# Two VectorE passes of an attention layer trade places around the z1 remainder

## The reference

```python
def layer(h, p):
    q = _phi(h @ wq + bq_)            # _phi(t) = elu(t) + 1
    k = _phi(h @ wk + bk_)
    v = h @ wv + bv_
    kv = einsum('bshd,bshm->bhdm', k, v)
    z = 1.0 / (einsum('bshd,bhd->bsh', q, k.sum(axis=1)) + 1e-06)
    att = einsum('bshd,bhdm,bsh->bshm', q, kv, z)
    h = _ln(h + att @ wo + bo_, g1_, be1_)
    y = gelu(h @ w1 + c1_) @ w2 + c2_
    return _ln(h + y, g2_, be2_)
xn = _layernorm(x)
out = x + attention_stack(xn) * silu(experts(xn))
```

## Time and profile before

| | us |
|---|---|
| median of three runs | 862.58 (862.35 to 863.84) |
| the profiled execution, device time | 865.69 |
| its span in the trace | 863.9 |
| TensorE busy in the span | 814.1 (94%) |
| VectorE busy | 777.9 (90%) |
| ScalarE busy | 736.0 (85%) |
| GpSimd busy | 407.6 (47%) |

### The profile page before, as it was taken

One profiled execution on the slowest core, in us unless ns is written; L12 is line 12 of the kernel. 1 busy time (PEld: TensorE's weight loads), 2 busy tenths in 40 slices (PEclk: granted clock), 3 DMA queues, 4 the chain that ended last, 5 costly groups with the idle time before them and its releaser, 6 DMA issues.

```text
span 863.9 us, 19249 instructions
## 1 busy us (share of the span) xinstructions
PE 814.1 (94%) x5914; PEld 738.6 (85%) x5914; DVE 777.9 (90%) x2675; ACT 736.0 (85%) x1315; POOL 407.6 (47%) x392
## 2 busy tenths in 40 slices
PE   5698999999999999999999999999999999998837
PEld 4588899999999999999999999999999999987624
DVE  6888999989899899989899899989899899998698
ACT  2579899989998899989999899989998899889734
POOL 5233454445544455344544445344544445465482
PEclk9799999999999999999999999999999999999985
DMA  5300200001010100001010100001010000000011
GB/s 147 89 2 2 44 2 18 18 16 30 2 35 2 44 2 22 14 17 28 2 34 2 45 1 24 12 18 27 2 35 2 1 1 2 12 15 1 2 38 61
DMA packets 26264, 18.76 MB, mean 22 GB/s; under 512 B 4354, under 2 KB 22195, under 8 KB 26164
## 3 DMA queue, kind: packets, MB, share of 16 engines
q1 hardware_dynamic: 25300, 16.95, 7.3%
q10 hardware_dynamic: 864, 0.59, 0.2%
HBM read 15.43 MB, written 2.10 MB: 20 GB/s over the span
## 4 chain that ended last, share of the span: by engine, by line
PE 80%; DVE 10%; ACT 7%; issue 3%; DMA 0%; ACTq 0%; DVEq 0%
PE down_ps L764 20%; PE small_ps L697 6%; PE att_ps L727 6%; PE up_ps L754 5%; PE up_ps L756 5%; PE up_ps L755 5%; PE t_ps L675 5%; PE t_ps L734 4%; PE kq_ps L687 3%; PE kq_ps L688 3%; PE kq_ps L689 3%; DVE z_lo L1042 3%; ACT z_hi L915 2%; PE up_ps L718 2%; PE small_ps L705 2%
## 5 line engine op out<-in xcount | busy, mean ns | idle before, releaser
L764 PE MATMUL down_ps<-w_use,hid 128*128 128x128 f32 x2048 | 259.8, 275 | 1.2 <-DVE h L1007 1.0
L764 PEld LDWEIGHTS down_ps<-w_use,hid 128*128 128x128 f32 x2048 | 244.0, 192 | 2.4 <-issue 2.0
L1060 POOL TENSOR_TENSOR res_ffn<-z_tm,g_ffn 128x512 f32<-128x512 f32 x64 | 81.9, 1279 | 249.4 <-DVE k_e L1173 237.9
L1049 POOL TENSOR_TENSOR res_att<-z_tm,g_att 128x512 f32<-128x512 f32 x64 | 82.5, 1288 | 154.4 <-DVE h L1000 154.4
L866 ACT ACTIVATE hid<-up_ps 128x512 f32<-128x512 f32 x192 | 113.3, 592 | 22.3 <-PE up_ps L756 14.8
L1012 DVE BATCH_NORM_STATS2 st<-h 128x6 f32<-128x128 f32 x504 | 107.1, 273 | 0.1
L921 ACT ACTIVATE z_tm<-h,shift,rstd 128x128 f32<-128x128 f32 x244 | 99.9, 483 | 0.0
L754 PE MATMUL up_ps<-z_hi,w_hi 128*128 128x512 f32 x192 | 86.5, 450 | 3.4 <-ACT hid L866 3.4
L1063 POOL TENSOR_TENSOR res_ffn<-res_ffn,ffn_row 128x512 f32<-128x512 f32 x64 | 84.1, 1314 | 5.0
L1052 POOL TENSOR_TENSOR res_att<-res_att,att_row 128x512 f32<-128x512 f32 x64 | 82.3, 1286 | 5.0
L687 PE MATMUL kq_ps<-w_kq_hi,zq_hi 128*128 128x256 f32 x256 | 82.0, 320 | 1.5 <-DVE zq_lo L958 1.5
(11 more groups left out here) (211 smaller groups left out, 2013.7 us busy)
## 6 DMA issues: line engine op xcount, KB each, us to landing
raw_w<-in_L_attn_W SPq DMA_DIRECT2D x15, 256.0 KB, 4.4
out_y<-gate_tm SPq DMA_DIRECT2D x8, 256.0 KB, 2.0
bias_bc<-in_L_attn_c SPq DMA_DIRECT2D x7, 256.0 KB, 4.7
x_tm<-in_L_attn_x SPq DMA_DIRECT2D x3, 512.0 KB, 7.2
raw_rows<-in_L_attn_be SPq DMA_DIRECT2D x15, 64.0 KB, 4.1
raw_g<-in_L_attn_g SPq DMA_DIRECT2D x14, 64.0 KB, 3.1
x_tm<-in_L_attn_x SPq DMA_DIRECT2D x2, 256.0 KB, 3.3
raw_rows<-in_L_attn_bo SPq DMA_DIRECT2D x8, 64.0 KB, 3.8
```

Source lines behind the costliest of these rows:

```text
L764: last = nc.tensor.matmul(down_ps[:, t, :], hid[:, j, t * P:(t + 1) * P], w2_use[:, j, :], start=(j == 0), stop=(j == FC - 1))
```

## The change

In each step VectorE takes the queries' last pass ahead of the z1 remainder, where the keys' floor pass stood, and the keys' floor pass behind the z1 remainder. No instruction is added or removed, and the lists of the other engines stay as they were.

```diff
@@ -1306,9 +1306,11 @@
                 dve_q_n(dve, p)
                 dve_kvo(dve, p)
             if proj:
-                dve_k_floor(dve, p + 1)
+                dve_q_elu(dve, p + 1)
             if ln1:
                 dve_z1_lo(dve, p - 1)
+            if proj:
+                dve_k_floor(dve, p + 1)
             if b == 1 and in_layers(l, 1, L - 1):
                 dve_w1_lo(dve, l)
             if proj:
@@ -1317,8 +1319,6 @@
                 dve_h2(dve, p - 2, b)
             if in_layers(l, 1, L - 2) and b in ZF_TILES and is_unit(p):
                 dve_zf(dve, l, ZF_TILES[b])
-            if proj:
-                dve_q_elu(dve, p + 1)
             if ffn:
                 dve_stats_of(dve, h2[:, b % 2], TT, s["h2_s"], p - 1, "st2_s")
```

## The result

The changed kernel takes **875.8 us** (median of 4 runs, 875.36 to 876.13); the kernel before, on the same chip, 863.21 (4 runs, 862.35 to 863.97). The ratio is 1.0146, 95% interval 1.0128 to 1.0163: the change costs 12.6 us, where 10.7 were forecast. The profiled execution took 876.13 us, with a span of 874.4, which is 10.5 longer than that of the profiled execution before (863.9).

What follows compares the result with a forecast made beforehand. TensorE was taken to set the time, VectorE counting only where TensorE waits. Six middle layers +6.3, first and last layer +3.0 and start +1.4 made +10.7 us, added to the 862.58 median: 873.3. Range: from rival 1 (865.9) up to 877.

Steps and rivals of the forecast that it cites:

- The floor pass is GpSimd's starting gun: Every step: the floor pass's end releases GpSimd's L1060 and L1063, 2.6 us of work, so the change moves them.
- Rival 1: b=2 and b=6: both zf tiles go through before L1063 starts, turning +0.92 into a gain; 865.9 us, chance 0.11.
- Rival 2: GpSimd's new place doesn't matter, so only the saving and half the start's cost remain; 860.0 us, chance 0.07.
- Rival 3: z1_lo comes late in every step and L675 waits for it; about 5 us more, 878; chance 0.10 with rival 4.
- Rival 4: q_exp is too late, so q_elu waits and the change doesn't do what it says; 878, chance 0.10 with rival 3.
- b=2, +0.50: Middle layers, step b=2: GpSimd's later passes hold both zf tiles, so the statistics and L705 come 0.50 us later.
- b=6, +0.42: Middle layers, step b=6: the same zf pair is held, with L705 already waiting; +0.42 us.
- b=3, +0.36: Middle layers, step b=3: lv ends 0.52 us later, held by GpSimd; 0.16 of that is cushion, leaving +0.36 us.
- b=1, -0.24: Middle layers, step b=1: w1_lo starts before L1060 and isn't held; TensorE gains the 0.24 us it waits.
- First and last layer, +3.0: Five holds of small passes and zf, +2.5 us (bounds 1 and 4), and late q_exp in four layer-0 steps, +0.5.
- The start, +1.4: First sequences: q_elu goes first, L1049 catches the floor pass, k_phi comes 2.4 us later; +1.4, bounds +0.3 and +2.5.

Runs made afterwards that it cites:

- old_late: Kernel before, VectorE's order kept; in the middle layers GpSimd's res_ffn passes released by k_phi's end instead of the floor pass: 881.46 us, ratio 1.0214.
- gate_zf: Changed kernel; in b=2 and b=6 of the middle layers GpSimd's res_ffn also waits until both zf tiles are written: 870.18 us, ratio 1.0083.
- zf_first: Kernel before with the changed order only in b=1, 2, 6 of the middle layers, zf directly behind the floor pass in b=2, 6: 869.19 us, ratio 1.0058.
- zf_late: Kernel before; in the middle layers zf moved behind q_elu in b=2, 6, and GpSimd's res_ffn waits for w1_lo in b=1: 862.86 us, ratio 0.9991.
- old_gate: Kernel before; in the middle layers GpSimd's res_ffn also waits for both zf tiles in b=2, 6 and for w1_lo in b=1: 862.5 us, ratio 0.9981.
- start: Kernel before with the changed order only in the first two steps (p = -1 and 0): 866.37 us, ratio 1.0017.
- gate_h2: Changed kernel; in b=2 and b=6 of the middle layers GpSimd's res_ffn also waits for h2: 874.48 us, ratio 1.0125.
- new_early: Kernel before with the changed order in the middle layers, where GpSimd's res_ffn is released by kvo's end instead of the floor pass: 871.95 us, ratio 1.0095.

## Why the prediction was right, and where its terms were off

**The mechanism.** *The floor pass is GpSimd's starting gun.* Shown: L1060 at z+1.19 in the trace after, and *old_late*, where moving the gun alone costs 18.5 us. *VectorE's tensor_scalar and tensor_tensor passes that touch no PSUM stand still beside GpSimd*: shown by the ends of zf, 0.08 or 0.09 after a GpSimd pass in four kernels, and by *gate_zf*, where the pair falls to 0.60. Rival 1, that both tiles slip in, is ruled out by the 1.65 in the trace after, and more sharply by *zf_first*. By start times the Trainium skill ("SBUF — State Buffer", "Who interferes with whom") would give a pass the ports for its whole length if it issues first. For one instruction the traces agree: w1_lo, which began 0.26 ahead of L1060, kept its 0.69 us, and L1060 was the one to stretch (the last section has the rows). For two queued ones the runs show that GpSimd gets its turn between them. Rival 2 would have needed no effect of GpSimd's place; *old_late* rules it out. Rival 3 was priced at 5 us more; L675's wait grew by 1.2 in total. Rival 4, q_elu waiting for q_exp, holds in layer 0, as in the sum; in the middle layers q_elu waits 0.19 to 0.30 us in one step a layer, and no step is longer by it.

**b=2, +0.50 forecast.** The statistics were late by exactly that, and the step is longer by 0.44 to 0.46. **b=6, +0.42**: measured 0.41 to 0.42.

**b=3, +0.36**: measured 0.26 to 0.27. lv took 0.68 from 469.48, ending at z+3.85 as forecast, and L705 waits 0.42:

```profile
469.48 0.68 DVE L194 TENSOR_SCALAR lv<-layer_vecs 128x4 f32<-128x4 f32 x1
...
472.25 0.30 PEld L705 LDWEIGHTS small_ps<-g_sb,w_v 128*128 128x128 f32 x2 [0.42 <-DVE g_sb L1123]
```

**b=1, -0.24**: measured -0.09 to -0.10. L705's wait vanished as forecast, but the gain was smaller. w1_lo's own length is 0.69 and not the 0.55 of the working: that was how far behind L1060 it ended, and a held pass ends sooner behind GpSimd than its own length (last section). It changed nothing, as VectorE had the time.

The last two have one reason, and it is the step of the working that failed: a load's wait was counted in full as TensorE's lost time. L705 is a weight load. When nothing holds it, it starts ahead of its own matmul, beside the matmul of L756, so that part of a wait is covered by that matmul. The rows show it in *zf_late* (z = 442.91), where L705 doesn't wait, and below them the same matmul of L706 in the changed kernel (z = 453.81):

```profile
448.46 0.39 PE L756 MATMUL up_ps<-z_lo,w_hi 128*128 128x512 f32 x1
448.47 0.41 PEld L705 LDWEIGHTS small_ps<-g_sb,w_v 128*128 128x128 f32 x2
448.91 0.39 PE L706 MATMUL small_ps<-g_sb,mean_f 128*128 128x128 f32 x2
...
460.27 0.39 PE L706 MATMUL small_ps<-g_sb,mean_f 128*128 128x128 f32 x2
```

L706's matmul, the next work behind, starts at z+6.00 in the first and at z+6.46 in the second: 0.46 for a wait of 0.62. With the step without that wait as the base, each case comes to wait - 0.15, within 0.02, and L706 is late by the same amount within 0.01:

```
step, kernel        wait of L705   step   base   cost   L706's matmul
b=1 before              0.24      11.90  11.81   0.09   z+6.09
b=6 before              0.20      12.30  12.25   0.05   z+6.05
b=3 after               0.42      12.72  12.46   0.26   z+6.27
b=2 after               0.62      12.27  11.81   0.46   z+6.46
b=6 after               0.61      12.71  12.25   0.46   z+6.46
b=3 old_late            0.69      13.00  12.46   0.54   z+6.54
```

The bases are of *zf_late* (b=1, 2, 6) and of before (b=3). In b=2 and b=6 of *old_late*, +1.3, a second wait comes ahead of it: TensorE's kq_ps matmuls wait for q_elu, which there stands behind the held zf. The middle layer came out as forecast (+1.04 on average in the layers without the odd step) since the errors cancelled: -0.10 in b=3 and -0.05 in b=2, +0.14 in b=1. That the layer fits to a hundredth is luck; that b=2 and b=6 carry it isn't. The same 0.15 explains why *old_gate* and *zf_late* found so little: the waits that they removed were mostly cover.

**First and last layer, +3.0**: measured 1.96 in layer 0 and 0.27 in the last, 2.2. All four passes that were named in layer 0 are held, each for 0.52 to 0.56 us longer than before. mr_x and lv took 0.15 before, r_f 0.17, and the last zf, four tiles, went from 1.10 to 1.66:

```profile
60.73 0.67 DVE L389 TENSOR_TENSOR mr_x<-mv_x,r_x 128x12 f32<-128x12 f32 x1
...
74.05 0.69 DVE L194 TENSOR_SCALAR lv<-layer_vecs 128x4 f32<-128x4 f32 x1
...
88.20 0.71 DVE L423 TENSOR_TENSOR r_f<-r_xn,r_x 128x32 f32<-128x32 f32 x1
```

The steps b=3, 4 and 6 grew by 0.65, 0.64 and 0.56: the hold, and in b=3 and 4 about 0.1 of the late q_exp. But in b=2, with mr_x held as well, the step grew by 0.12 only (13.21 to 13.33), so that hold was cushioned; the lower bound of this term had allowed for such cases. In the last layer L540 took 0.52 instead of 0.22, L705 behind it waited 0.93 instead of 0.65, and the step took 0.29 more.

**The start, +1.4**: *start* measured +1.5. The unit-1 marks of the traces lie at 53.7 us on average in nine traces with the old order there and at 55.7 in four with the new (54.4 to 57.6), +2.0. L1049 held the floor pass and k_phi came late:

```profile
17.13 1.26 POOL L1049 TENSOR_TENSOR res_att<-z_tm,g_att 128x512 f32<-128x512 f32 x1
...
17.29 1.39 DVE L1173 TENSOR_SCALAR k_e<-k_e 128x512 f32<-128x512 f32 x1
18.71 0.69 DVE L1180 SCALAR_TENSOR_TENSOR k_phi<-kq_ps,k_e 128x512 f32<-128x512 f32 x1
...
22.24 0.17 DVE L194 TENSOR_SCALAR lv<-layer_vecs 128x4 f32<-128x4 f32 x1
```

k_phi stands 2.71 later than in the earlier trace rows (forecast 2.4; in this execution q_exp already came 0.10 later and L1049 0.29 later than there), and lv, no longer held, took 0.17 instead of 0.87, as forecast.

**What is left over.** 1.96, 6.46, 0.27 and a start of 1.5 to 2.0 make 10.2 to 10.7, and the two profiled spans differ by 10.5, so the sum of 10.7 agrees with the traces. In part that is luck again: the first and last layer were taken 0.8 too high, the start perhaps 0.1 to 0.6 too low, and the odd step of one layer wasn't in the sum. The four runs against four gave 12.6, with a lower end of the interval at 11.0; against the 863.86 of 23 later runs of the kernel before it would be 11.9. The start varies by 3.7 us between traces of one order, enough for the difference, but which part of the changed kernel, if any, adds the last 1 to 2 us isn't settled: the stretches behind unit 1 don't have it.

## What to carry to other kernels

Before moving a pass, ask who is released by it: here an edit on VectorE moved 2.6 us of GpSimd's work per step about 1.3 us later or more, onto VectorE's own SBUF passes in three steps of eight, and *old_late* and *gate_zf* show from two sides that this was the price. A second engine that shares SBUF has a place in time that must be planned: put it beside passes that read PSUM, and expect that whatever moves it off one victim puts it on the next (den_e, w1_lo, the floor pass). Count the wait of a weight load less what the matmul before it covers, 0.15 us for this load, and compare executions by stretches between fixed marks, since a start that varies by 3.7 us hides a gain of 0.8.

## What the runs showed of the hardware

- Two VectorE passes back to back don't keep GpSimd out. When GpSimd's pass was ready 0.26 us after the first tile had begun, the second tile waited for the whole GpSimd pass (*zf_first* and *gate_h2*, 1.61 and 1.62 us for a pair of 0.60).
- The hold goes both ways: GpSimd's L1060, normally 1.28 us, took 1.58 beside w1_lo, which had begun 0.26 before it:

```profile
442.93 0.69 DVE L229 TENSOR_TENSOR w_lo<-fold_w,w_hi 128x512 fp32r<-128x512 f32 x1
...
443.19 1.58 POOL L1060 TENSOR_TENSOR res_ffn<-z_tm,g_ffn 128x512 f32<-128x512 f32 x1 [5.18 <-DVE k_e L1173]
```

- A held pass ends behind GpSimd by less than its own length, and the longer it is, the further: lv (0.15 us by itself) ended 0.02 behind it, zf's tile (0.34) 0.08, the floor pass (0.42) 0.27 (b=5 of *new_early*), w1_lo (0.69) 0.55.
- Small passes are held too: lv, 128x4, for 0.53 us, and L540, 8x8, for 0.30. Statistics (0.28 us), reductions (0.65) and passes with an operand in PSUM (k_phi 0.69) took as long beside GpSimd as without it in the trace after, though the first two touch SBUF alone.
